# A one-core vision block: key and query transfers split over two DMA queues, with a new order of work on every engine

## The reference

```
p = img2patches(x); h = layernorm(p) @ W + b; h = layernorm(h)          # 196 tokens x 192
h = h + attn(_layernorm(h))       # 12 heads of 16, causal, with a relative-position term, softmax, projection
h = h + ffn(_layernorm(h))        # below
# ffn: scores = sigmoid(normed @ Wr + br); the 15% of tokens with the lowest scores (29) get full attention,
#      the others normed + scores * pooled, times Wm; then h + merged, a layer norm, gelu(n2 @ W1) @ W2, residual
```

## Time and profile before

| | |
|---|---|
| median of 3 runs | 4954.72 us (4946.73 to 4960.03) |
| the profiled execution | 4944.02 us, of which the span from first to last instruction is 4942.2 us |
| PE busy | 4696.2 us (95%) |
| PEld busy | 4299.3 us (87%) |
| DVE busy | 3872.3 us (78%) |
| ACT busy | 3448.9 us (70%) |
| POOL busy | 3065.9 us (62%) |
| mean granted TensorE clock | 0.989 of full speed |
| DMA, all queues | 340.16 MB, mean 69 GB/s |

### The profile page before, as it was taken

How to read it: one execution, slowest core, us unless ns; L and a number is a source line. 1 busy time by engine, 2 the same in 40 slices (tenths; PEclk the granted TensorE clock), 3 DMA queues, 4 the chain that set the end, 5 groups by cost and what they waited for, 6 DMA issues and landing times. The chain is left out here.

```text
span 4942.2 us, 143405 instructions
## 1 busy us (share of the span) xinstructions
PE 4696.2 (95%) x44376; PEld 4299.3 (87%) x44376; DVE 3872.3 (78%) x13015; ACT 3448.9 (70%) x12030; POOL 3065.9 (62%) x4143
## 2 busy tenths in 40 slices
PE   3899999999999999999999999999999999999998
PEld 3788888888888888888888888888888888888887
DVE  3787887887888788788788878878878877887885
ACT  1667777776776777777677677777777767767775
POOL 2566666666666666666666666666666666666664
PEclk7899999999999999999999999999999999999999
DMA  5555555455555555555555555555554555555551
GB/s 70 68 68 72 69 71 72 66 74 67 69 73 67 72 70 70 72 67 73 69 67 74 67 70 72 68 72 69 71 71 66 74 67 69 72 67 72 70 70 21
DMA packets 339085, 340.16 MB, mean 69 GB/s; under 512 B 47652, under 2 KB 306033, under 8 KB 339057
## 3 DMA queue, kind: packets, MB, share of 16 engines
q1 hardware_dynamic: 332522, 337.37, 52.3%
q10 hardware_dynamic: 6535, 2.45, 0.3%
HBM read 204.78 MB, written 19.27 MB: 45 GB/s over the span
## 5 line engine op out<-in xcount | busy, mean ns | idle before, releaser
L1610 ACT ACTIVATE p<-banks,negmax 98x98 f32<-98x98 f32 (+1 forms) x3072 | 1139.3, 379 | 216.9 <-issue 121.8
L544 POOL TENSOR_TENSOR p<-p,rden 98x392 f32<-98x392 f32 x1152 | 980.9, 870 | 280.8 <-DVE rden L1242 280.7
L1226 DVE TENSOR_REDUCE negmax<-banks 98x2 f32<-98x392 f32 (+1 forms) x1152 | 609.6, 557 | 141.0 <-PE banks L732 122.2
L732 PE MATMUL banks<-kz,qparts 128*98 128x392 f32 x2304 | 648.9, 385 | 0.0
L1610 ACT ACTIVATION_READ_ACCUMULATOR p<-banks,negmax 98x1 f32 x3072 | 612.0, 199 | 0.0
L743 PE MATMUL banks<-tokw,x_sb 128*98 128x193 f32 x3072 | 592.4, 336 | 15.5 <-POOLq L556 14.6
L743 PEld LDWEIGHTS banks<-tokw,x_sb 128*98 128x98 f32 x3072 | 553.9, 252 | 20.3 <-issue 14.6
L767 PE MATMUL banks<-ident,p 98*98 98x98 f32 x4608 | 530.4, 252 | 24.1 <-ACTq L1614 4.1
L695 PE MATMUL banks<-z3Ts,w_split 128*128 128x196 f32 x3840 | 508.4, 279 | 33.7 <-ACT gT L1685 32.3
L695 PEld LDWEIGHTS banks<-z3Ts,w_split 128*128 128x128 f32 x3840 | 468.2, 192 | 64.2 <-ACT gT L1685 58.0
L535 POOL TENSOR_TENSOR gparts<-gT,gparts 128x392 fp32r<-128x392 f32 x384 | 395.2, 1040 | 190.9 <-DVE gparts L1434 190.9
(11 more groups left out here) (264 smaller groups left out, 11542.3 us busy)
## 6 DMA issues: line engine op xcount, KB each, us to landing
x_sb<-in_x SPq DMA_DIRECT2D x384, 196.0 KB, 5.0
kz<-kq SPq DMA_DIRECT2D x1024, 73.5 KB, 2.6
x_sb<-in_x SPq DMA_DIRECT2D x256, 190.8 KB, 8.9
x_sb<-in_x SPq DMA_DIRECT2D x256, 185.5 KB, 11.1
qparts<-kq SPq DMA_DIRECT2D x256, 147.0 KB, 2.7
x_sb<-in_x SPq DMA_DIRECT2D x128, 189.0 KB, 7.3
out<-out_row SPq DMA_DIRECT2D x128, 147.0 KB
pT<-in_L_ffn_W ACTq DMA_DIRECT2D x1, 576.0 KB
```

What stands on the lines that cost most here:

```text
L544: gp.tensor_tensor(heads, heads, rden[:, g, t, s0:s0 + sn].unsqueeze(2).broadcast_to([HT, sn, w]), ALU.mult).then_inc(sem["pnorm_sb"], 1)
L732: last = mm(o, qparts[:, g, HT * t:HT * t + HT], kz[:, slots[0]:slots[-1] + 1, part, g, 0:w], start=False, stop=part == 1, skip_group_chec ...
L1226: ve.tensor_reduce(negmax[:, g, t, slots[0]:slots[-1] + 1], bank[RING[f"S{k}"]][0:HT, 0:w * len(slots)].rearrange("p (s w) -> p s w", w=w) ...
L1610: sc.activation((p1 if t else p0)[0:HT, 4 * g + s], bank[b][0:HT, w * i:w * i + w], ACT.Exp, bias=negmax[:, g, t, s:s + 1], accum_out=den[ ...
```

## The change

The ten transfers are halved between two queues. SP keeps the four kz transfers into partitions 0 to 63 and the first qparts transfer; ScalarE gets a `place_keys` of its own, which waits for kqlo_sb and issues the other four and the second qparts transfer. Sizes, semaphores and their counts stay. Beside it, all four compute engines have their calls in a new order. The core of the diff (the second `place_keys` is ScalarE's):

```
-                for s in range(4):
-                    for r in range(2):
-                        at = 64 * r + DH * s
-                        sp.dma_start(kz[at:at + DH, s].bitcast(F32),
-                                     kq[DH * s:DH * s + DH].bitcast(F32)).then_inc(
-                                         sem["kz_in"], 16)
-                for part in range(2):
-                    sp.dma_start(qparts[64 * part:64 * part + 64].bitcast(F32),
-                                 kq[64:128, part].bitcast(F32)).then_inc(sem["q_in"], 16)
+                for s in range(4):
+                    at = slice(DH * s, DH * s + DH)
+                    sp.dma_start(kz[at, s].bitcast(F32), kq[at].bitcast(F32)).then_inc(
+                        sem["kz_in"], 16)
+                sp.dma_start(qparts[0:64].bitcast(F32),
+                             kq[64:128, 0].bitcast(F32)).then_inc(sem["q_in"], 16)
...
+                def place_keys():
+                    sc.wait_ge(sem["kqlo_sb"], after("kqlo_sb", l))
+                    if not front:
+                        sc.wait_ge(one["stores_zeroed"], 1)
+                    for s in range(4):
+                        at = 64 + DH * s
+                        sc.dma_start(kz[at:at + DH, s].bitcast(F32),
+                                     kq[DH * s:DH * s + DH].bitcast(F32)).then_inc(
+                                         sem["kz_in"], 16)
+                    sc.dma_start(qparts[64:128].bitcast(F32),
+                                 kq[64:128, 1].bitcast(F32)).then_inc(sem["q_in"], 16)
...
-                    gelu(2)
-                if front:
-                    attention()
                 if head:
                     keys()
+                    place_keys()
```

More of the change, by code:

```diff
@@ L585, in step @@
                 if back:
+                    gp.drain()
+                    gp.tensor_tensor(h2b[:], h2[:], both(bf2), ALU.add).then_inc(sem["h2b_sb"], 1)
+                if head:
+                    gp.wait_ge(sem["tok_var"], after("tok_var", l))
+                    rstd(var1[:], ve1[:], rstd1[:], "tok_rstd")
+                if back:
                     gp.wait_ge(sem["rden2_sb"], after("rden2_sb", m))
@@ L619, in step @@
                         sem["f_rstd"], 1)
+                if back:
+                    gp.wait_ge(sem["h3_stat"], after("h3_stat", m))
+                    rstd(mv_3[:, :, 1], ve5[:], rstd5[:], "h3_rstd")
                 if back:
@@ L984, in attention_cols @@
                     rows_to_cols(2, a_row, "aT_mm")
+                if front:
+                    values()
                 if back:
@@ L988, in step @@
                 if front:
-                    values()
+                    causal("S0")
                 if tail:
@@ L992, in step @@
                 if back:
+                    score()
+                if front:
+                    causal("S1")
+                if back:
                     keys2()
-                    score()
+                if front:
+                    causal("S2")
+                    causal("S3")
+                if back:
+                    values2()
+                    mixing_rows()
+                if front:
+                    causal("S4")
+                if back:
+                    gather()
+                    weighted_sum()
+                if front:
+                    causal("S5")
+                    causal("S6")
+                if back:
+                    qsel()
                 if head:
@@ L1057, in step @@
                     attention()
+                if head:
+                    keys()
+                if front:
+                    projection()
+                if tail:
+                    down(0)
                 if back:
                     scatter()
-                if front:
-                    projection()
-                if head:
-                    keys()
                 if tail:
-                    down(0)
                     down(1)
@@ L1532, in step @@
                     attention()
+                if head:
+                    keys()
+                if front:
+                    residual()
                 if back:
@@ L1693, in step @@
                     load_table(ACT.Exp)
+                if head:
+                    squares()
                 if back:
@@ L1696, in step @@
                     exp_scores()
-                if head:
-                    squares()
-                if tail:
-                    mlp_cols_hi()
+                if front:
+                    softmax(0)
                 if back:
@@ L1708, in step @@
                 if front:
-                    softmax(2)
                     softmax(3)
@@ L1725, in step @@
                 if front:
+                    transposed("A1")
+                if tail:
+                    gelu(0)
+                if front:
                     transposed("B0")
                 if tail:
-                    load_table(ACT.Gelu)
-                    gelu(0)
                     gelu(1)
```

143 lines of the change are left out of this document (57 added, 86 removed).

## The result

| | before | after |
|---|---|---|
| median of four runs, us | 4954.15 (4946.73 to 4960.03) | 5394.27 (5393.3 to 5395.18) |
| ratio | | 1.0889 [1.0876, 1.0902] |
| span of the profiled execution, us | 4942.2 | 5392.9 |
| TensorE idle per step, us | 1.11 | 3.76 |
| step, us | 37.39 | 40.95 |

The kernel became 440 us slower. The direction was forecast; the 5028 us were not, and the range ended at 5110.

What follows compares the result with a forecast made beforehand. TensorE sets the pace, only its idle time can be won. Idle of 1.70 instead of 1.11 us a step adds 74 us to 4944.0, giving 5018, plus 10.7 for the median: 5028 us; 8 in 10 range 4950 to 5110.

Steps and rivals of the forecast that it cites:

- The fifth starts at 7.85 and lands at 10.55: Each queue's fifth transfer, with issues of 0.62 us from 5.33 and 2.7 us from issue to landing.
- So S0 waits for 0.5 us: TensorE is ready for S0 1.24 us into the step, the transfers land at V + 1.75.
- The release: Both queues can start issuing at T + 5.33, 2.0 us earlier than before, once DVE's low part is done.
- rival 1: Transfers land late, at up to T + 12.3, limited by DMA engine time: 5093 to 5185 us, chance 0.2.
- The forecast ones: TensorE's old waits for gelu and at context2 were to go; the projection's was put at 0.25 instead of 0.23 us.
- TensorE's own work stays 36.28 us: No compute instruction is added or dropped, so TensorE's busy time per step stays 37.39 - 1.11 us.
- The walk behind S0: DVE's list delays nTs to 12.05, so score starts at 12.1 with 1.05 us of idle TensorE, S0's wait inside it.
- DVE's wait for h3_rstd: DVE waits at z3 from 9.0 to 10.1, 1.1 us, because POOL does h2 before h3_rstd.
- The projection's 0.25 us: TensorE waits for yparts before the projection, from 3.65, for 0.25 us instead of 0.23.
- my sum: Idle of 1.70 us a step instead of 1.11, so +0.59 us over 125 steps: 74 us.
- the small waits: Two or three new TensorE waits of about 0.1 us (S4, gather, A4), 0.3 us a step, held at 0 to 1.
- ScalarE's issues: 3.1 us of issues from 5.33 to 8.45 on ScalarE, covered by 0.8 us ahead of nTs, cost nothing.

Runs made afterwards that it cites:

- The filled wait: The changed kernel with twenty small transposes put on TensorE ahead of S0's wait for the transfers: 5225.82 us, 1.0562.
- last experiment: Changed kernel with S0 and S1 behind keys2, square sums first and output ahead of z3, plus GpSimd's residual sum waiting for z3: 5065.2 us, 1.0239.

## Why the prediction was wrong

**The step that failed** is "The fifth starts at 7.85 and lands at 10.55", and with it "So S0 waits for 0.5 us". The release was right (T + 5.42 against 5.33). The fifth issue starts 0.5 us late, for 0.67 to 0.73 us an issue, and the landing of 2.7 us, taken from a trace with one queue at work, is 3.6 to 3.8 with two. S0 starts at T + 12.42, where rival 1's long end had 12.3. I had worked that landing out from the DMA share of the earlier trace rows and then gave it 0.2, for a reason (one queue had reached a share over 1) that does not bear on these transfers. That its 12.3 fits so well is in part luck: between the first bytes and S0 lie 5.9 us, as in its 5.1 + 0.8, but the DMA engines' share over them is 0.80, so 4.7 us of engine time and not 5.1 at a share of 1. In the loop's window S0 waits for 61.3 us in 24 steps, 2.55 us each: 125 x 2.55 = 319 us.

**A term was missing in every case**, rival 1 included: what the wait does to the clock. Its 5185 us carry the late transfers, and the result is 209 us above. The filled wait prices the lower clock behind the S0 waits at 168 us. Together 319 + 168 = 487 us; the measured difference is 440, so all the rest of the change gives back 47 us. It is not TensorE's other waits that give it back. The forecast ones did go (0.23 at the projection in the earlier trace rows, the gelu, context2), but new ones came, so that idle time outside S0's wait is 3.76 - 2.55 = 1.21 us a step, against 1.11. What fell is busy time: 37.4 us a step in the filled run, of which 1.7 are the filler, so 35.7 to 35.8 against 36.28. My "TensorE's own work stays 36.28 us" was wrong by that half microsecond. Why, no run shows.

**The Trainium skill's rule** in "DMA: Bandwidth & Descriptors", section "Rules for kernel authors", is that transfers to disjoint partition halves serialize and two issuers save only issue time. The runs agree with it. The rival that I tied to it had the last landing at T + 12.3, and in the step shown it is at about 12.2 (8.36 + 3.8); halving the bytes brings S0 1.25 us earlier. That does not make the second queue useless: one queue alone has S0 at T + 14.1, so the split is worth 1.7 of the 3.1 us of issues. Weighing the rival at 0.2 was the mistake.

**The walk behind S0 was partly right, and hidden.** DVE's wait for h3_rstd is 0.69 us (1.1 forecast, from 9.0 to 10.1), nTs ends at T + 11.72 (12.05) and score starts at T + 11.78 (12.1) once S0 is out of its way. But what ends last there is not nTs: the transposes write the bank that the output of the image before is read from, so they wait for `out_row`, 1.39 us. In my walk the output add was only a step ahead of the subtractions. nTs comes just before score even so, and once the transposes wait less, 0.35 us of waiting for nTs shows (last experiment). The projection's 0.25 us does not occur. By my sum the orders should cost some 74 us; with S0 moved they cost 231.

**The rest of that is the small waits**, held at 0 to 1 us and taken as 0.3. The sigmoid's products wait for 0.77 us a step there, a stripe's transposes of p for 0.36 and the routing's for 0.23. The first is in part DVE's ez, held by GpSimd's normalisation and square sums, which in the old orders did not meet it. No walk with durations of the old trace could show that: the duration itself depends on what stands beside it. Undoing two of these meetings brought the time from 5178 to 5065 us, the second of them through the clock.

**ScalarE's issues** were rightly put at nothing in the new orders: f0 is released by the shift, and the high part of nTs is ready 0.45 us before DVE takes it up, where 0.8 us of cover were forecast. In the old orders the issues cost 588 us, the lower clock included.

## What to carry to other kernels

A transfer's landing time read with one queue at work is not its landing time with two: before moving a reader up to a split transfer, work out the bytes over the DMA engines' share and take the later of the two times. TensorE's waits of 2.6 us cost their length here and half as much again in clock (319 and 168 us). Waits of 1.4 to 1.5 us cost clock too, but only in some steps, 30 of 116 and 44 of 118. So if a reader must be early, put other work ahead of it rather than let it wait, and compare busy time and granted clock as well as idle time before saying what an edit won. And when orders change, see which DVE and GpSimd operations newly meet, since their old durations no longer hold.

## What the runs showed of the hardware

- Two queues, each with five transfers from 16 or 64 partitions: kz lands in 3.3 us instead of 2.6, qparts in 3.6 to 3.8 instead of 2.7; with half the bytes in kz, kz lands in 2.0. Which rows are read makes no difference (1.0902 against 1.0889).
- A DMA issue holds ScalarE's stream for 0.73 us here, more than the 0.47 of the earlier trace rows and more than SP's 0.67.
- The granted clock falls from 2.4 to 1.2 GHz at 84 of 111 waits of 2.5 us, at 105 of 105 of 4.3 us, at 30 of 116 of 1.4 us, at 44 of 118 of 1.5 us and at none of 118 of 0.83 us. The length of the wait does not settle it: in the run with half the bytes it falls at none of 116 waits of 1.36 us at S0, and behind 22 of 116 of 0.8 us at the sigmoid. Behind one wait of 2.57 us it is 0.50 for over 5 us, behind the next, of 2.46 us, it stays at 1.00.
- Some DVE operations end only when GpSimd's does. One step of the change, DVE and GpSimd:

```profile
2082.45 0.78 DVE L1317 TENSOR_SCALAR ez<-ez 98x2 f32<-98x2 f32 x1
...
2084.68 2.00 DVE L1331 SCALAR_TENSOR_TENSOR f<-mrow,keep,f 98x192 f32<-98x192 f32 x2
```

```profile
2082.03 1.19 POOL L560 TENSOR_TENSOR gstore<-gstore 128x588 f32<-128x588 f32 x1
```

The small DVE operation ends at 2083.23, GpSimd's at 2083.22. Not every meeting is like that: the two statistics of h2 take 0.35 us each beside GpSimd's instructions in before and 0.35 without any beside them in the change. The Trainium skill, page "SBUF — State Buffer", section "Who interferes with whom", says that the two share a pair of ports that only some DVE instructions need, and that of two instructions that need it the later one is fully blocked until the other's whole instruction ends. The trace agrees, in this step and at z3 (0.67 us alone, 1.36 beside the residual sum).
